# Output bias by copies and accumulating DMAs in DRAM, a difference form of token mixing, a ring of three tiles, and the first late norm on ScalarE

## What is computed

```
x  = layernorm(x + attn(x))            # 16 heads of width 16
x  = layernorm(x + ffn(x))

attn: q, k, v = x@Wq+bq, x@Wk+bk, x@Wv+bv
      sparsity = max(scores) - mean(scores)   # per query, over all 4096 keys
      the 307 queries of a head with the highest sparsity get softmax(q k^T) v, all others 0
      attn = out @ Wo + bo
ffn:  x_prev = x shifted by one token (zeros in front)
      xr = mu_r*x + (1-mu_r)*x_prev ;  xk = mu_k*x + (1-mu_k)*x_prev
      ffn = sigmoid(xr @ W_r^T) * (square(relu(xk @ W_k^T)) @ W_v^T)
```

## Time and profile before

| | us |
|---|---|
| median of 3 runs | 3242.62 (3241.13 to 3245.9) |
| the profiled execution | 3246.53 |
| its span in the trace | 3244.8 |
| PE, DVE, ACT, POOL busy in the span | 2945.3, 2894.6, 2821.5, 1611.0 |
| late feed, first output product to last store | about 3088 to 3243 |

### The profile page before, as it was taken

How to read it: one execution, slowest core, us unless ns; L and a number is a source line. 1 busy time by engine, 2 the same in 40 slices (tenths; PEclk the granted TensorE clock), 3 DMA queues, 4 the chain that set the end, 5 groups by cost and what they waited for, 6 DMA issues and landing times. The chain is left out here.

```text
span 3244.8 us, 56078 instructions
## 1 busy us (share of the span) xinstructions
PE 2945.3 (91%) x14524; PEld 1334.2 (41%) x14524; DVE 2894.6 (89%) x5704; ACT 2821.5 (87%) x6214; POOL 1611.0 (50%) x2867
## 2 busy tenths in 40 slices
PE   6999899998999999999899999899998799897588
PEld 3333333333433433443343444444444343344376
DVE  4999999999989998998999999899998698997567
ACT  5999898998999999999899888799997699895476
POOL 4223022224645554653364566766546464657754
PEclk8999999999999999999999999999999999998889
DMA  6324223241251242123111252122241212202122
GB/s 183 92 84 119 74 72 86 86 41 34 44 42 29 37 42 36 21 39 36 35 37 44 51 46 51 38 39 36 42 48 38 46 33 20 42 17 16 19 84 74
DMA packets 276909, 166.61 MB, mean 51 GB/s; under 512 B 182188, under 2 KB 256108, under 8 KB 272492
## 3 DMA queue, kind: packets, MB, share of 16 engines
q1 hardware_dynamic: 268492, 159.56, 26.0%
q0 software_dynamic: 6144, 1.37, 0.5%
q10 hardware_dynamic: 1952, 2.10, 0.2%
HBM read 111.86 MB, written 47.86 MB: 49 GB/s over the span
## 5 line engine op out<-in xcount | busy, mean ns | idle before, releaser
L1185 DVE CUSTOM_DVE_ANT_0 JK<-DP,AB 128x1024 bf16<-128x1024 f32 x2048 | 2459.6, 1222 | 215.2 <-DVE SPr L1185 88.6
L1035 ACT ACTIVATE AB<-CP 128x512 f32<-128x512 f32 x4096 | 2292.1, 623 | 188.5 <-PE CP L782 131.1
L801 PE MATMUL DP<-KS,QS 128*128 128x512 f16 x4096 | 1233.5, 383 | 69.1 <-DVE SPr L1185 60.8
L1673 POOL TENSOR_TENSOR SCR<-E 128x307 f16<-128x307 f32 x957 | 665.1, 708 | 491.4 <-ACT E L1064 485.4
L782 PE MATMUL CP<-KS,QS 128*128 128x512 f16 x2048 | 791.4, 386 | 56.3 <-ACT AB L1035 33.0
L791 PE MATMUL CP<-KS,QS 128*128 128x512 f16 x2048 | 792.2, 387 | 36.3 <-ACT AB L1035 0.2
L801 PEld LDWEIGHTS DP<-KS,QS 128*128 128x128 f16 x4096 | 354.4, 99 | 368.7 <-DVE SPr L1185 179.1
L1064 ACT ACTIVATE E<-BP 128x307 f32<-128x307 f32 x896 | 428.5, 478 | 40.3 <-PE BP L862 34.4
L782 PEld LDWEIGHTS CP<-KS,QS 128*128 128x128 f16 x2048 | 197.6, 96 | 532.8 <-ACT AB L1035 457.9
L791 PEld LDWEIGHTS CP<-KS,QS 128*128 128x128 f16 x2048 | 196.8, 96 | 421.1 <-ACT AB L1035 375.2
L862 PE MATMUL BP<-QT,KA 128*128 128x307 f16 x896 | 265.7, 297 | 12.4 <-DMA QT<-SCR 8.6
(11 more groups left out here) (411 smaller groups left out, 3016.9 us busy)
## 6 DMA issues: line engine op xcount, KB each, us to landing
KS<-KTC SPq DMA_DIRECT2D x256, 128.0 KB
QS<-QSC SPq DMA_DIRECT2D x512, 64.0 KB
KA<-KTC SPq DMA_DIRECT2D x128, 128.0 KB
QN<-SCR SPq DMA_DIRECT2D x16, 544.0 KB, 3.4
SCR<-in_L_attn_x SPq DMA_DIRECT2D x16, 512.0 KB, 5.1
AO<-E SPq DMA_DIRECT2D x16, 512.0 KB, 6.8
VF<-in_L_attn_x SPq DMA_DIRECT2D x64, 128.0 KB, 2.1
VF<-AO SPq DMA_DIRECT2D x64, 128.0 KB, 2.2
```

Source lines behind the costliest of these rows:

```text
L801: r = pe.matmul(o[:, 512 * j:512 * j + 512], qs, ks[j][:, 0, :], start=True, stop=True)
L1035: act.activation(AB[p % 3][:, 512 * j:512 * j + 512], BANK["C%d" % j], ACT.Abs).then_inc(ab_full, 1)
L1185: dve.tensor_tensor_reduce(out=JK[p % 2][:], in0=BANK["D%d" % u], in1=AB[p % 3][:], scale=1.0, scalar=0.0, op0=ALU.add, op1=ALU.max, accum ...
L1673: pool.tensor_tensor(EL[a % NE], E[a % NE][:], EH[a % NE], ALU.subtract).then_inc(el_g, 1)
```

## The change

1. The bias leaves the feed. A DRAM tensor Y per sequence gets a copy of x by 16 DMAs that SP issues in `values(0)` (`ycopy`), 512 KB each, DRAM to DRAM. In `tokens(1)` POOL issues 16 DMAs of 512 KB that add the bias tile bob to Y (`ybias`); all of them wait for the 16 copies. f0 loads fx from Y. L1726 goes, and DVE waits in f2 for the load itself.
2. Token mixing is written x_prev + mu*(x - x_prev). One difference fd for both halves, and then per half one scaling by mu and one sum with x_prev: on POOL one difference, four scalings, two sums; late on DVE one difference and four fused instructions. ACT's four scalings (L1101) and their wait go.
3. x1T becomes one strip of 3 x 128 + 1 columns. The last column of a tile is the shifted first of the next, so the copy of it (L1095) is needed for every third tile only.
4. The late f3 moves from DVE to ACT; POOL makes its offset as it did early (one more 128x1 instruction in f2r).

```diff
--- before.py
+++ after.py
@@ tokens
-                yield waiting + [("xt", b, c, k, bk)] + ... + ([("xload", b, c + 4)] if k and c < 4 else [])
+                yield (waiting + [("xt", b, c, k, bk)] + ... + ([("xload", b, c + 4)] if k and c < 4 else [])
+                       + ([] if fast else [("ybias", k, c)]))
@@ values
-                yield step + ([("azero", t // 16, t // 2 % 8)] if b == 0 and t % 2 + part == 0 else [])
+                yield step + ([("azero", t // 16, t // 2 % 8)] if b == 0 and t % 2 + part == 0 else
+                               [("ycopy", t // 16, t // 2 % 8)] if b == 0 and (t % 2, part) == (1, 1) else [])
@@ tiles
+        def x1_of(k, shift):
+            a = 128 * (k % 3) + shift
+            return x1R[:, :, a:a + 128]
@@ scalar f4
-                q = seq.mark(act.copy(x1T[k % 3][:, :, 1:129], sv))
-                act.copy(x1T[(k + 1) % 3][:, :, 0:1], sv[:, :, 127:128]).then_inc(f_x1T, 1)
+                if k % 3 == 2:
+                    act.copy(x1R[:, :, 0:1], sv[:, :, 127:128])
+                act.copy(x1_of(k, 1), sv).then_inc(f_x1T, 1)
+
+            def f3(b, t, late):
                 if late:
-                    act.wait_ge(q_act, q)
-                    after(act, f_mx, k)
-                    for m, cb in enumerate((MR1, MK1)):
-                        for c in range(2):
-                            act.mul(fmp[m][:, c, :], x1T[k % 3][:, c, 0:128], ...).then_inc(f_fmp, 1)
+                    k = NT * b + t
+                    r = frs[:, k % 2, :]
+                    after(act, f_o2, k - 3)
+                    after(act, f_t1, k - 3)
+                    act.wait_ge(f_r1, k + 1)
+                    act.activation(fx1[k % 4], fh[k % 2], ACT.Identity, scale=r[:, 0:1], bias=r[:, 1:2]).then_inc(f_x1, 1)
@@ vector f2
-                dve.wait_ge(f_xb, k + 1)
+                dve.wait_ge(l_f[k % 3], 32 * (k // 3 + 1))
@@ vector f5 (late; f3 removed)
-                    dve.wait_ge(f_fmp, 4 * (late_of[b, t] + 1))
+                    q = seq.mark(dve.tensor_tensor(fd[k % 2], cur, prv, ALU.subtract))
+                    dve.wait_ge(q_dve, q)
...
-                            i = dve.scalar_tensor_tensor(out=fm[:, c, :], in0=cur[:, c, :],
+                            i = dve.scalar_tensor_tensor(out=fm[:, c, :], in0=fd[k % 2][:, c, :],
                                                          scalar=cols[:, ca.start + c:ca.start + c + 1],
-                                                         in1=fmp[m][:, c, :], op0=ALU.mult, op1=ALU.add)
+                                                         in1=prv[:, c, :], op0=ALU.mult, op1=ALU.add)
@@ gpsimd
+            def ybias(b, i):
+                pool.wait_ge(l_y, 256)
+                pool.dma_start(Y[b][512 * i:512 * i + 512, :].rearrange("(t p) c -> p t c", p=128),
+                               bob[:].unsqueeze(1).broadcast_to([128, 4, D]), accum_op=ALU.add).then_inc(l_yb, 16)
@@ gpsimd f1
-                pool.wait_ge(l_f[k % 3], 32 * (k // 3 + 1))
-                pool.tensor_tensor(fx[k % 3], fx[k % 3], bob[:], ALU.add).then_inc(f_xb, 1)
@@ gpsimd f5 (early)
+                pool.wait_ge(q_pool, seq.mark(pool.tensor_tensor(fd[k % 2], cur, prv, ALU.subtract)))
...
                     for c in range(2):
-                        pool.tensor_scalar(fmp[m][:, c, :], prv[:, c, :], cols[...], 0.0, ALU.mult, ALU.add)
-                        i = pool.tensor_scalar(fm[:, c, :], cur[:, c, :], cols[...], 0.0, ALU.mult, ALU.add)
+                        i = pool.tensor_scalar(fm[:, c, :], fd[k % 2][:, c, :], cols[...], 0.0, ALU.mult, ALU.add)
                     pool.wait_ge(q_pool, seq.mark(i))
-                    i = pool.tensor_tensor(fm, fm, fmp[m], ALU.add)
+                    i = pool.tensor_tensor(fm, fm, prv, ALU.add)
@@ sync
+            def ycopy(b, i):
+                sp.dma_start(Y[b][512 * i:512 * i + 512, :], x[b][512 * i:512 * i + 512, :]).then_inc(l_y, 16)
@@ sync f0
-                sp.dma_start(fx[i], x[b][128 * t:128 * t + 128, :]).then_inc(l_f[i], 16)
+                sp.dma_start(fx[i], Y[b][128 * t:128 * t + 128, :]).then_inc(l_f[i], 16)
```

More of the change, by code:

```diff
@@ L92, in tokens @@
                 state["late"] = None if fast else bk
-                yield waiting + [("xt", b, c, k, bk)] + (evict if fast else []) + ([("xload", b, c + 4)] if k and c < 4 else [])
+                yield (waiting + [("xt", b, c, k, bk)] + (evict if fast else []) + ([("xload", b, c + 4)] if k and c < 4 else [])
+                       + ([] if fast else [("ybias", k, c)]))
                 waiting, state["late"] = [] if fast else evict, None
@@ L445, in attention_rwkv @@
         KTC = nc.dram_tensor("KTC", [NB, 2, D, 3 * L // 2], F16, kind="Internal").ap()
-        QN, AO = ([nc.dram_tensor(f"{n}{b}", [L, w], F32, kind="Internal").ap() for b in range(NB)]
-                  for n, w in (("QN", H * (DH + 1)), ("AO", D)))
+        QN, AO, Y = ([nc.dram_tensor(f"{n}{b}", [L, w], F32, kind="Internal").ap() for b in range(NB)]
+                     for n, w in (("QN", H * (DH + 1)), ("AO", D), ("Y", D)))
         IDX = nc.dram_tensor("IDX", [len(GROUPS), 8, 16 * A_COLS], I32, kind="Internal").ap()
@@ L562, in attention_rwkv @@
                 "D00": DP[:, 0, 0:512], "D01": DP[:, 0, 512:1024], "D10": DP[:, 1, 0:512], "D11": DP[:, 1, 512:1024]}
-        BQ, BK, MR, MK, SH, MR1, MK1, KB = (slice(2 * i, 2 * i + 2) for i in range(8))
-        l_w, l_c, l_z, l_m, l_i, l_q = (sem(n) for n in ("l_w", "l_c", "l_z", "l_m", "l_i", "l_q"))
+        BQ, BK, MR, MK, SH, KB = (slice(2 * i, 2 * i + 2) for i in range(6))
+        l_w, l_c, l_z, l_m, l_i, l_q, l_y, l_yb = (sem(n) for n in ("l_w", "l_c", "l_z", "l_m", "l_i", "l_q", "l_y", "l_yb"))
         l_p = [sem(f"l_p{i}") for i in range(6)]
@@ L605, in attention_rwkv @@
         el_of = {"G": el_g, "D": el_d}
-        late_of = {k: i for i, k in enumerate(token[1:3] for token in plan if token[0] == "f4" and token[4])}
+        def x1_of(k, shift):
+            a = 128 * (k % 3) + shift
+            return x1R[:, :, a:a + 128]
         wraw = {"k": W2["k"][:], "q": QS[:, 0:1024].bitcast(F32).rearrange("p (k n) -> p k n", k=2),
@@ L1381, in f2 @@
                                          op0=ALU.add, op1=ALU.add, accum_out=fsum[:, j:j + 1]).then_inc(f_y, 1)
-            def f3(b, t, late):
-                if late:
-                    k = NT * b + t
-                    j = k % 2
-                    after(dve, f_o2, k - 3)
-                    after(dve, f_t1, k - 3)
-                    dve.wait_ge(f_r1, k + 1)
-                    dve.tensor_scalar(fx1[k % 4], fh[j], fnm[:, j:j + 1], frs[:, j, 0:1], ALU.add,
-                                      ALU.mult).then_inc(f_x1, 1)
             def f5(b, t, late):
@@ L1702, in f2r @@
                 pool.wait_ge(q_pool, seq.mark(pool.tensor_scalar(r[:, 0:1], fssq[:, j:j + 1], 1.0 / D, EPS, ALU.mult, ALU.add)))
-                i = pool.tensor_tensor(r[:, 0:1], r[:, 0:1], halfc[:], ALU.pow)
-                if not late:
-                    pool.wait_ge(q_pool, seq.mark(i))
-                    i = pool.tensor_tensor(r[:, 1:2], fnm[:, j:j + 1], r[:, 0:1], ALU.mult)
-                i.then_inc(f_r1, 1)
+                pool.wait_ge(q_pool, seq.mark(pool.tensor_tensor(r[:, 0:1], r[:, 0:1], halfc[:], ALU.pow)))
+                pool.tensor_tensor(r[:, 1:2], fnm[:, j:j + 1], r[:, 0:1], ALU.mult).then_inc(f_r1, 1)
             def rstd(q, late):
@@ L1744, in f5 @@
                 pool.wait_ge(f_x1T, k + 1)
[L1745 removed]
+                pool.wait_ge(q_pool, seq.mark(pool.tensor_tensor(fd[k % 2], cur, prv, ALU.subtract)))
+                for m, ca in enumerate((MR, MK)):
                     fm = (fm0, fm1)[m][k % 2]
                     for c in range(2):
[L1748 to L1750 removed]
+                        i = pool.tensor_scalar(fm[:, c, :], fd[k % 2][:, c, :], cols[:, ca.start + c:ca.start + c + 1], 0.0,
                                                ALU.mult, ALU.add)
                     pool.wait_ge(q_pool, seq.mark(i))
[L1753 removed]
+                    i = pool.tensor_tensor(fm, fm, prv, ALU.add)
                 i.then_inc(f_mx, 1)
@@ L1909, in f0 @@
                     sp.wait_ge(pv_pe, NT * H)
+                    sp.wait_ge(l_yb, 256)
                     after(sp, f_o3, NT * b)
@@ L1919, in f9 @@
                 sp.dma_start(out[b, 128 * t:128 * t + 128, :], fo[k % 4]).then_inc(l_out[k % 4], 16)
-            stages = dict(xload=xload, rest=rest, azero=azero, split=split, qstore=qstore, head=head, qload=qload, sel=sel, ixdma=ixdma, ka=ka, qt=qt, f0=f0, f9=f9)
+            stages = dict(xload=xload, rest=rest, azero=azero, ycopy=ycopy, split=split, qstore=qstore, head=head, qload=qload, sel=sel, ixdma=ixdma, ka=ka, qt=qt, f0=f0, f9=f9)
             first = [args for stage, *args in plan if stage == "xload"][:4]
```

33 lines of the change are left out of this document (12 added, 21 removed).

## The result

The changed kernel takes 3221.36 us (median of 4 runs, 3219.1 to 3223.93) against 3243.14 of the kernel before: 21.8 us less, ratio 0.9928 (0.9913 to 0.9944). The forecast was 9.5 us less, 3233, and its range ended at 3226. All runs together, these and those made later beside the experiments, give 3241.5 before (65 runs, 3232.4 to 3252.7) and 3221.6 after (10 runs, 3218.9 to 3226.5), 19.9 us less. So the sign was right and the gain is twice what was forecast.

What follows compares the result with a forecast made beforehand. DVE bounds the main loop, a DVE-POOL loop the late feed, PE close behind. Late 5, early 4.5 and transfers 0 make 9.5 us less, 3242.62 to 3233; own range 3226 to 3236, with rivals 3226 to 3245.

Steps and rivals of the forecast that it cites:

- Late feed, 5 us less: Late feed: norm on ACT cuts the DVE-POOL loop, PE binds at 4.02 us a trip; 5 less, between 0 and 8.
- Early feed, 4.5 us less: Early feed: POOL's shorter trips shrink waits of ACT and PE that reach DVE; 4.5 us less, between 0 and 9.
- The share: Early feed: in one row 2.85 of 5.03 us of ACT's wait reached DVE, so a little over half counts.
- The size: Early feed, POOL: mixing 4.4 to 3.8 us and bias sum 0.72 gone, so the mean comes 1.3 us earlier.
- The list: Early feed: waits of ACT for POOL's mean and of PE for its mixing, shrinking by 8.7 us together.
- The upper bound of 9 us: Early feed: the most it could gain, 9 us, if DVE finds no other waits.
- Transfers at 0: New copies and accumulating DMAs cost 0, hidden if POOL issues each within 4.16 us before the second sequence's first split.
- 1: Late feed: the loop stays above PE's pace; at 4.2 us a trip the total is 3238; chance 0.15.
- the difference that waits for a power: Late feed, DVE: the new difference waits out POOL's 0.57 us power, trip 4.07, total 3234.5; a quarter within the forecast.
- 2: First split of the second sequence: POOL not free in time, slower; at 5 us a DMA 3246.5; chance 0.17.
- 3: Early feed: gain does not count, stalls come back at the next place; late alone 3238; chance 0.11.
- What the profile was to show: Early ACT waits for the mean under 9 us, POOL 42 less busy; first split near 407, ACT eviction at its place.

Runs made afterwards that it cites:

- y_only: Kernel before with Y made and loaded, so no bias sum on POOL; old mixing, late norm still on DVE: 3223.39 us, ratio 0.9953.
- mix_only: Kernel before with the difference form of mixing and the ring of three tiles; bias sum on POOL and late norm on DVE kept: 3223.74 us, ratio 0.9952.

## Why the prediction was wrong, point by point

- **What bounds the kernel**: right. DVE carries the main loop, a loop of DVE and POOL the late feed, with PE close behind.
- **Late feed, 5 us less**: right that the loop is cut and PE binds, and nearly right in size, 3.7 by the mean of three traces. The trip is 3.99 (forecast 4.02) and late loads take some back. Which part brings it was wrong: either of two steps would have done, and the forecast put it on the norm. The row that said so was quoted in its own text, the norm at 0.71 beside the bias sum and 0.41 without.
- **Early feed, 4.5 us less**: this is the step that failed; it measured 14.5. The mechanism was right, POOL's shorter trips reach DVE through the waits of ACT and PE, but three terms of the sum were too small. *The share.* "By the row, 2.85 of 5.03 reached DVE, so a little over half counts": shortening came through whole, 1.75 and 1.83. The waits listed were 8.7 us, and by a factor of 1 the sum would have been 8.7. *The size.* 1.3 us a trip was 1.44: the old mixing was priced right (4.4), the new one at 3.8 where it takes 3.67, since its difference ran 0.61 and its sums 0.68, not 0.72. *The list.* Only waits that the profile puts on POOL's mean and mixing were counted. The largest one left out is a wait of PE for the running sums of the selection, which POOL makes behind mixing and bias sum. The waits of the two kernels, in the stretches of the earlier trace rows and of the kernel after, have it as
```profile
PE BP L839 <- POOL lower_half L1597: 5.6, 1, 5.6
```

```profile
PE BP L845 <- POOL lower_half L1599: 4.2, 1, 4.2
```

  At the start of head 27 it is 5.63 to 5.68 us in the three traces of the kernel before, 4.17 in all three of the kernel after, 4.96 in `y_only` and 4.88 in `mix_only`; the main loop gained some 1.5 us there. The remaining 4 us or so beyond the 8.7 are spread over heads 21 to 27 and have not been followed to single waits. DVE's idle time also shows up under other names. In the timeline of the kernel before, a listed wait of ACT of 0.50 us is followed by an idle time of DVE that is put down to DVE itself, and in the kernel after 0.16 of its 0.78 is left:
```profile
1872.99 0.51 ACT L1084 ACTIVATE VF<-VF,fnm 128x256 bf16<-128x256 f32 x1 [0.50 <-POOL fnm L1695]
...
1874.69 1.22 DVE L1185 CUSTOM_DVE_ANT_0 JK<-DP,AB 128x1024 bf16<-128x1024 f32 x1 [0.78 <-DVE SPr L1185]
```

```profile
1877.87 1.23 DVE L1193 CUSTOM_DVE_ANT_0 JK<-DP,AB 128x1024 bf16<-128x1024 f32 x1 [0.16 <-DVE SPr L1193]
```

- **The upper bound of 9 us** was that same list taken whole, so it was no bound. What POOL is freed of, 1.3 us times the trips, 35 to 42 us, would have been a bound that holds the result.
- **Transfers at 0**: right, with some 5 us of cover left.
- **Rivals**: 1 fell (3.99 a trip), and with it the difference that waits for a power: it runs 0.42 us in the mean of 26 late trips. 2 fell (0.9985 to 1.0016 for the transfers), 3 fell (14.5).
- **What the profile was to show**: ACT's waits for the mean under 9 us (9.6), POOL 42 us less busy (50.5), the first split near 407 (409.75, with a main loop that began 2.2 later), the eviction at its place (419.98, was 417.51, the same shift). Apart from ACT's waits, a little over 9, all about as said, and yet the gain was twice the forecast: the signs named were those of its mechanism, and none measured how much of it reached DVE.

## What to carry to other kernels

When an engine waits on a chain that the bound engine stands behind, don't price a shortening by the share of the wait that got through today: the covered part comes first and the exposed part last, so each us taken off counts whole until the exposed part is gone. Take (time freed a trip) x (trips) as the mark from above for such a gain, look for every engine that waits on the freed one and not only for the instructions that were changed, and expect a curve that bends, half and then a fifth here, so that two edits of equal size are not worth twice one. And where a loop holds an instruction that a neighbour slows, removing the neighbour may free the loop before anything is moved.

## What was not expected of the hardware

- A row of 15 accumulating DMAs of 512 KB leaves POOL at 1.3 us each, and the next issue holds POOL 39.8 us, until the fifteenth has landed.
- An activation of 128x256 took 0.60 us with scale and bias read from SBUF, 0.42 with constants.
- A DVE instruction of 0.35 us took 4.7 to 4.9 us in 3 of 17 traces, beside POOL's unbroken row of work.
- The same DVE norm took 0.67 us beside a POOL sum of 128x256 and 0.41 without it.
